# Prologue of a fused attention and expert block: key weights and tables loaded ahead of the query weights, two steps moved on the engines

## What is computed

```python
mod = (_silu(c) @ wmod).reshape(B, 6, 1, -1)          # six rows for each sequence
sa, ca, ga, sb, cb, gb = (mod[:, i] for i in range(6))
h = _layernorm(x) * (1 + ca) + sa
fused = h @ w_kv_a                                    # 192 query, 64 key, 64 rotary columns
q = _rmsnorm(q_c, q_a_gamma) @ w_qb                   # 16 heads, 128 plain and 64 rotary columns
kv = _rmsnorm(kv_c, kv_a_gamma) @ w_kvb
q_pe = q_pe * cos + _rotate_half(q_pe) * sin
scores = einsum('bqhd,bkhd->bhqk', q_full, k_full) * scale      # causal, softmax follows
x = x + ga * (attn.reshape(b, s, NH * DV) @ w_o)
```

## Time and profile before

| what | value |
|---|---|
| median of three runs | 1194.12 us (1193.44 to 1194.33) |
| the profiled execution, its own time | 1192.75 us |
| its span, first to last instruction | 1190.9 us |
| mean granted clock of TensorE | 0.981 of 2.4 GHz |
| busy: PE, PEld, DVE, ACT, POOL | 93%, 72%, 66%, 53%, 40% of the span |

### The profile page before, as it was taken

How to read it: one execution, slowest core, us unless ns; L and a number is a source line. 1 busy time by engine, 2 the same in 40 slices (tenths; PEclk the granted TensorE clock), 3 DMA queues, 4 the chain that set the end, 5 groups by cost and what they waited for, 6 DMA issues and landing times.

```text
span 1190.9 us, 20543 instructions
## 1 busy us (share of the span) xinstructions
PE 1108.2 (93%) x6444; PEld 862.2 (72%) x6444; DVE 780.3 (66%) x2404; ACT 628.1 (53%) x1840; POOL 477.9 (40%) x524
## 2 busy tenths in 40 slices
PE   6699999999999999999999999999999999998792
PEld 3488777877688767877687768887688768885471
DVE  3567658774787568775777568775777378764541
ACT  2367635765377535764377625763476626762120
POOL 1223114651455324650455234641555234532364
PEclk8899999999999999999999999999999999999896
DMA  9353404450345104540345114530354114530893
GB/s 303 119 123 77 85 1 121 128 125 1 89 107 142 37 18 124 131 100 1 88 116 133 36 34 109 146 85 1 89 139 115 33 40 107 133 78 19 252 227 37
DMA packets 87551, 114.62 MB, mean 96 GB/s; under 512 B 16346, under 2 KB 51096, under 8 KB 87456
## 3 DMA queue, kind: packets, MB, share of 16 engines
q1 hardware_dynamic: 68416, 98.56, 32.8%
q0 software_dynamic: 7168, 6.20, 2.7%
q10 hardware_dynamic: 11872, 8.65, 2.6%
HBM read 35.56 MB, written 15.11 MB: 43 GB/s over the span
## 4 chain that ended last, share of the span: by engine, by line
PE 62%; DVE 16%; ACT 5%; issue 5%; POOL 5%; DMA 3%; SPq 2%; ACTq 1%; POOLq 0%; DVEq 0%
PE PS L816 11%; PE PS L795 9%; PE PS L776 5%; PE PS L775 5%; PE PS L774 5%; PE PS L974 3%; DVE probs L1408 3%; PE PS L945 3%; PE PS L805 2%; PE PS L924 2%; PE PS L926 2%; PE PS L744 2%; PE PS L746 2%; PE PS L745 2%; PE PS L748 2%
## 5 line engine op out<-in xcount | busy, mean ns | idle before, releaser
L1153 ACT ACTIVATE probs<-probs,nmax 128x512 f32<-128x512 f32 (+3 forms) x512 | 283.3, 554 | 170.7 <-DVE nmax L1408 167.8
L1408 DVE CUSTOM_DVE_ANT_0 probs<-PS,cmask 128x512 f32<-128x512 f32 (+3 forms) x512 | 229.3, 487 | 90.8 <-PE PS L776 90.6
L774 PE MATMUL PS<-kTh,qT 128*128 128x512 f32 (+3 forms) x512 | 177.0, 346 | 5.2 <-DMA qT<-qstage 5.2
L1162 ACT ACTIVATE pT<-PS 128x384 f32<-128x384 f32 (+3 forms) x320 | 125.3, 454 | 80.6 <-PE PS L795 80.6
L776 PE MATMUL PS<-kTh,qT 128*128 128x512 f32 (+3 forms) x512 | 165.8, 324 | 0.0
L775 PE MATMUL PS<-kTl,qT 128*128 128x512 f32 (+3 forms) x512 | 165.3, 323 | 0.0
L569 POOL TENSOR_TENSOR qr<-qr 128x512 f32<-128x512 f32 x64 | 81.5, 1274 | 206.5 <-DVE qr L1394 206.3
L795 PE MATMUL PS<-ident,probs 128*128 128x128 f32 x1280 | 158.4, 275 | 5.7 <-DVE nmax L1408 3.3
L795 PEld LDWEIGHTS PS<-ident,probs 128*128 128x128 f32 x1280 | 139.6, 140 | 19.8 <-issue 14.4
L816 PE MATMUL PS<-pT,kmat 128*64 128x512 f32 (+3 forms) x1024 | 152.0, 439 | 0.3 <-issue 0.3
L631 POOL DMA_INDIRECT tab_dram<-entry,slot x112 | 111.6, 996 | 33.1 <-issue 27.3
(11 more groups left out here) (254 smaller groups left out, 1808.7 us busy)
## 6 DMA issues: line engine op xcount, KB each, us to landing
qT<-qstage SPq DMA_DIRECT2D x128, 256.0 KB
qT<-qstage SPq DMA_DIRECT2D x256, 128.0 KB
x_in<-in_x SPq DMA_DIRECT2D x8, 512.0 KB, 4.0
modb<-mod_dram SPq DMA_DIRECT2D x8, 512.0 KB, 4.6
h_dram<-mod_dram SPq DMA_DIRECT2D x8, 512.0 KB, 9.3
h_dram<-h SPq DMA_DIRECT2D x8, 512.0 KB, 3.3
out<-base SPq DMA_DIRECT2D x8, 512.0 KB, 3.5
pT<-in_wo SPq DMA_DIRECT2D x1, 2048.0 KB, 10.9
```

Of the source, the lines that this page charges most:

```text
L774: pe.matmul(PS[:, bank, 0:n], qh, kTh[:, 0:n], start=True, stop=False)
L1153: act.activation(probs[:, UO[u]:UO[u] + UW[u]], probs[:, UO[u]:UO[u] + UW[u]], ACT.Exp, scale=-1.0, bias=nmax[:, u:u + 1], accum_out=psums ...
L1162: cp = act.activation(pT[:, h, 0:i + 1, bass.ts(i, P)], PS[:, bank, col:col + UW[u]].rearrange("p (j q) -> p j q", q=P), ACT.Copy)
L1408: dve.tensor_tensor_reduce(out=probs[:, UO[u]:UO[u] + UW[u]], in0=PS[:, SBANK[u], 0:UW[u]], in1=cmask[:, S - UW[u]:S], scale=-1.0, scalar= ...
```

## The change

Three edits, all of them in the prologue. SyncE issues the three loads of query weights behind the four rotary tables and not ahead of `wkva`. PE turns the modulation rows ahead of the absorption, and absorbs all 16 heads in one piece behind the wait for `wq_in`. ScalarE rounds the rotary half of pair 0 ahead of its copies of the output weights; in the later sequences that step keeps its place.

```diff
             sp.dma_start(x_in[:], rows(xr, 0)).then_inc(x_landed, 16)
-            for dst, src in ((wqn_st[:, :, 0:QL], wqnT), (wqn_st[:, :, QL:], wqnT[:, :, P:QL])):
-                sp.dma_start(dst, src.rearrange("h p n -> p h n")).then_inc(wq_in, 16)
-            sp.dma_start(wk_st, wkT).then_inc(wq_in, 16)
             sp.dma_start(wkva_sb[:], wkva.rearrange("(c p) n -> p c n", p=P)).then_inc(wk_in, 16)
...
             sp.dma_start(sinT_sb[:], sinT).then_inc(wk_in, 16)
+            for dst, src in ((wqn_st[:, :, 0:QL], wqnT), (wqn_st[:, :, QL:], wqnT[:, :, P:QL])):
+                sp.dma_start(dst, src.rearrange("h p n -> p h n")).then_inc(wq_in, 16)
+            sp.dma_start(wk_st, wkT).then_inc(wq_in, 16)
             sp.dma_start(wv_st, wvT).then_inc(wv_in, 16)
...
             turn_h1(0, 1, 7)
+            turn_modulation()
             pe.wait_ge(wq_in, 3 * 16)
-            absorb_query(0, range(0, NH // 2))
-            turn_modulation()
-            absorb_query(0, range(NH // 2, NH)).then_inc(wabs_ps, 1)
+            absorb_query(0, range(NH)).then_inc(wabs_ps, 1)
             middle(0, 0, False, True)
...
                 if not post:
+                    rotary_high(n, 0)
                     act.wait_ge(wvo_ps, 1)
...
-                if pre:
+                if pre and post:
                     rotary_high(n, 0)
```

## The result

The changed kernel took 1196.12 us as the median of 11 runs (1193.65 to 1199.28), the kernel before, run beside it 11 times, 1193.44 (1191.32 to 1198.65). The ratio is 1.0020 with a 95% interval of 1.0010 to 1.0029: 2.4 us slower, between 1.2 and 3.5. The forecast was 1195.8, 1.7 above the median it started from.

The account below looks back on a forecast made before the run. The prediction took the prologue's chain of waits, loads then hops between engines, to bound the kernel. Heads +7.3, rounding -3.7 and clock -1.9 gave +1.7, 1195.8 us; own range 1194.2 to 1197.9, with rivals 1191.9 to 1198.2.

Parts of the forecast that it names:

- The chain passes the prologue's sum on whole: Prologue: a microsecond won or lost ahead of the first score at 59.61 should reach the program's end whole.
- The loads swap, last landing at 24.9: Load queue: same bytes reordered, tables landing at 16.4 and query weights at 24.9 us.
- bound of 0.35: Load queue: the most a gap in the queue can add, 0.35 us, as table issues end after x_in lands.
- 16 heads at the lower level, 7.3: PE's absorption ahead of the key projection: 16 heads at the lower clock delay it by 7.3 us, bounds 3.68 and 7.4.
- warm rival: Absorption on PE: heads raise the clock after 3.3 us, loss 3.6, total 1192.1 us; chance 0.20.
- The projection, nothing: Key projection on PE: length stays 6.20 us, taken as no change, bounds -0.2 to +1.1.
- The rounding, -3.7: Pair 0's rotary half: rounding ahead of ScalarE's copies starts GpSimd's subtraction and the first score 3.7 us earlier.
- The clock term, -1.3 for this execution: First scores: shorter PE idle time, 1.45 us, avoids the clock's fall; 1.3 us gained here, 1.9 in a typical run.
- The sum: Whole program: +7.3 - 3.7 - 1.3 = +2.3 us against the profiled execution, +1.7 against the median.
- Cold scores: Rival at the first scores: clock gain of 1.9 becomes 0, total 1197.7 to 1198.8 us; chance 0.18.
- Nothing moves: Rival: query weights land earlier in a shorter queue or later work absorbs the difference, 1193 to 1195.5 us; chance 0.10.
- It doesn't do what it says: Rival: tables land ahead but no engine reads them sooner; counted as part of the forecast, no separate chance.

Follow-up runs that it names:

- the key weights ahead: The changed kernel with `wkT` loaded ahead of the two loads of `wqnT`, still behind the tables: 1195.51 us in one execution.
- eight and five warm products: The changed kernel with eight or five unread 128x512 products on PE before the query-weight wait: 0.9995 and 0.9991 of the kernel before.
- projection first: The changed kernel with the key projection ahead of all absorption heads on PE, weight splits moved behind: 0.9949 of the kernel before.

## Why the prediction was right

The median came out 0.3 from the forecast, and the direction, a small loss, was the one given. The costs stand where the prediction put them, on the heads and on the rounding; the nearness of the number is in part luck, as the sum shows. Step by step:

- *The chain passes the prologue's sum on whole:* shown. In each of ten traces (before, after and the eight experiments) it is 1015.5 to 1016.1 us from the first turned sums to L912 of the last sequence.
- *The loads swap, last landing at 24.9:* this is the term that was mis-sized. The last of the query and key weights landed at 26.04 in the changed kernel, 1.1 later than forecast, and between 25.8 and 25.9 in the four experiments with its load order. That is well outside the bound of 0.35, and more than the half microsecond that the prediction itself named as a sign of being wrong. The bound counted only a gap in the queue; none shows while the tables are loaded, and yet the tables took 1.4 us longer at their new place and landed at 17.75 instead of 16.4.
- *16 heads at the lower level, 7.3:* 7.09, at a granted clock of 0.5 throughout, and 7.09 again with the key weights ahead. The warm rival falls for this kernel. The Trainium skill (TensorE: Matmul & The Clock Gate, Part 1) says that activity releases the throttle. The projection did raise the clock, 3.5 us after it began; 7.09 us of heads on a full PE did not.
- *The projection, nothing:* 6.18 in the chain against 6.20. The places from there to L744 moved alike (8.15 and 7.92), so the splits of the weights were indeed hidden.
- *The rounding, -3.7:* from GpSimd's sum to its subtraction it is 0.73, as forecast, and before it was 4.41: the 3.7 are there. But at the first score only 3.2 of them are left (7.92 later at pair 0's products, 4.75 at the score), since the moves took 0.5 longer: 2.94 from the last issue where it was 2.45. The first of pair 0's latent moves is issued 2.06 ahead of the first rotary one now (57.19 and 59.25), before it was 5.74. Over all ten traces the two go together: 2.94 to 3.10 in the four with 2.06 to 2.08 between them (the changed kernel, eight and five warm products, projection first), 2.44 to 2.50 in the six with 2.7 or more. That the moves share the queue is the likely reason; it was not tried apart.
- *The clock term, -1.3 for this execution:* 10.17 from first score to turned sums and not 11.53, so 1.36. But the reason for it is weaker than the prediction had it. By the six rows at the end of the experiments, no fall came after 1.8 to 2.3 us of idle time ahead of the first score, and a fall after 2.6 to 3.0. The forecast had 1.5, and 1.8 came; but the idle time depends on how fast pair 0's and pair 1's products ran, so the term comes and goes with the prologue's clock. Nor does the idle time decide alone: at about 19.6 the changed kernel's clock fell only 0.4 us after PE's turns had ended.
- *The sum:* +2.3 was forecast against the profiled execution, and the first turned sums stand 3.39 later. The load's 1.1 and the moves' 0.5 were too little; 0.2 for the heads, 0.2 between the projection and pair 0's products, and 0.1 elsewhere too much. The median's +2.4 lies between this and the forecast's +1.7: the runs scatter by more than the load term is worth. That the median is only 0.3 off is in part luck: the kernel before had 1194.12 in the three runs that the forecast started from and 1193.44 in the eleven beside the change, from which the same +1.7 would have given 1195.1, 1.0 too low. The lower end of the forecast's own range, 1194.2, should by its bounds be 1194.4; nothing hangs on it.
- *Cold scores* did not happen in the changed kernel, but did in three of the experiments with the early rounding. There the fall cost about 1.6 us (11.73 to 11.79 from first score to turned sums, where the others with the early rounding have 10.17 to 10.20); the rival's term was 1.9.
- *Nothing moves* falls, since PE waited for the load until 26.09. *It doesn't do what it says* holds, as the forecast had it: the tables landed at 17.75, and the projection read them at 33.17.

## What to carry to other kernels

An early load is worth something only if the engine that uses it reaches its use earlier: look at what stands ahead of the use in that engine's order, and move that as well. Work that was hidden under a wait costs its full length, at the clock that the wait leaves behind, as soon as the wait moves ahead of it. In a chain of short steps, an operation whose result another engine waits for should stand ahead of bulk copies that wait for something else.

## What was not expected of the hardware

Granted clock and PE's idle time: short heads of 128x64 kept the upper level for 3.79 us when they found it, lost it in the kernel before at 21.5 us while PE was busy with them, and did not bring it back in 7.09 us in the changed kernel. Unread products in PE's idle time added to the rounding's gain: 7.3 us with them, 4.2 for the rounding alone, though the two intervals just overlap (5.5 to 9.2 and 2.5 to 6.0). And the same weights and tables, 2144 KB, took 6.84 us in one place of the load queue and 8.3 in another.
